# Weight loads in pieces of four row blocks, and the gate projection evacuated bank by bank, in an eight-core attention and expert-mixture layer

## What is computed

```
q, k, v, s, g = x @ Wq, x @ Wk, x @ Wv, clip(x @ Ws), x @ Wg
o = scan over tokens of (q, k, v, s)          # per head
o = o * rsqrt(mean(o*o) + eps) * g_norm_weight
o = o * (g * sigmoid(g))                       # the gate
x = layernorm(x + o @ Wo)
h = relu(x @ W1 + b1); alpha = softmax(h @ W2 + b2)
x = layernorm(x + sum_k alpha_k * U_k (V_k x))
```

## Time and profile before

| | |
|---|---|
| median of 2 runs | 1934.78 us (1932.53 to 1937.03) |
| profiled execution, its own time | 1948.56 us |
| its span, first to last instruction, core 7 | 1947.0 us |
| spans of the eight cores | 1908.6 to 1947.0 us |
| TensorE busy | 1357.1 us, 70% of the span |
| VectorE, ScalarE, GpSimd busy | 532.6, 409.1, 292.5 us |
| bytes read from HBM | 237.45 MB |

### The profile page before, as it was taken

How to read it: one execution, slowest core, us unless ns; L and a number is a source line. 1 busy time by engine, 2 the same in 40 slices (tenths; PEclk the granted TensorE clock), 3 DMA queues, 4 the chain that set the end, 5 groups by cost and what they waited for, 6 DMA issues and landing times.

```text
span 1947.0 us, 18988 instructions; the slowest of 8 cores (1908.6 to 1947.0 us)
## 1 busy us (share of the span) xinstructions
PE 1357.1 (70%) x6800; PEld 653.6 (34%) x6800; DVE 532.6 (27%) x886; ACT 409.1 (21%) x552; POOL 292.5 (15%) x310
## 2 busy tenths in 40 slices
PE   3358989969985554778685658967555477868562
PEld 1124444434433333333232323423333333324231
DVE  2013232341002222343421372000222234342135
ACT  0000000001124444320200131102444432020013
POOL 2100000001011111442111102201111144211100
PEclk9669999989985555887676868978555587768686
DMA  9940100015114000559935249961300055984502
GB/s 182 179 76 22 44 22 22 22 44 108 23 24 64 0 1 1 87 87 182 201 72 86 34 88 228 160 96 27 61 1 1 1 87 87 181 156 76 87 1 87
DMA packets 62956, 146.27 MB, mean 75 GB/s; under 512 B 8976, under 2 KB 13456, under 8 KB 57488
## 3 DMA queue, kind: packets, MB, share of 16 engines
q0 software_dynamic: 56240, 102.91, 34.7%
q1 hardware_dynamic: 5472, 33.76, 5.1%
q10 hardware_dynamic: 1152, 8.39, 1.1%
HBM read 237.45 MB, written 8.39 MB: 126 GB/s over the span
## 4 chain that ended last, share of the span: by engine, by line
PE 46%; DMA 19%; DVE 14%; ACT 8%; issue 6%; POOL 4%; DVEq 1%; ACTq 0%; another core or an unknown queue 0%; POOLq 0%
PE fb L245 44%; DMA wvb<-wv 5%; DMA wob<-wo 4%; DMA wkb<-wk 3%; DMA w1b<-w 3%; PE tb L245 2%; POOL wbf L265 2%; DMA wsb<-ws 2%; ACT rbuf L265 1%; DVE x1bufs L265 1%; DMA wqb<-wq 1%; DVE msq L265 1%; DVE st L265 1%; DVE sm L265 1%; ACT wrw L265 1%
## 5 line engine op out<-in xcount | busy, mean ns | idle before, releaser
L245 PE MATMUL fb<-w1b,x2fm 128*128 128x512 bf16 x512 | 140.6, 437 | 33.5 <-DMA w1b<-w 33.5
L245 PE MATMUL fb<-wob,ofm 128*128 128x512 bf16 x512 | 141.4, 450 | 14.1 <-DMA wob<-wo 14.1
L245 PE MATMUL fb<-wvb,xpf 128*128 128x512 bf16 x512 | 119.9, 395 | 32.7 <-DMA wvb<-wv 32.7
L245 PE MATMUL fb<-wgb,xmf 128*128 128x512 bf16 x512 | 132.7, 426 | 2.9 <-DVE psf L265 2.9
L245 PE MATMUL fb<-wvb,xmf 128*128 128x512 bf16 x512 | 118.5, 393 | 16.5 <-DMA wvb<-wv 16.5
L265 DVE TENSOR_TENSOR okb<-fb,rbuf 128x256 f32<-128x256 f32 x32 | 13.6, 424 | 316.3 <-ACT rbuf L265 171.4
L245 PE MATMUL fb<-wsb,xpf 128*128 128x512 bf16 x256 | 72.9, 449 | 31.4 <-DMA wsb<-ws 18.2
L245 PEld LDWEIGHTS fb<-w1b,x2fm 128*128 128x128 bf16 x512 | 53.0, 107 | 113.4 <-issue 82.8
L245 PEld LDWEIGHTS fb<-wob,ofm 128*128 128x128 bf16 x512 | 56.7, 112 | 97.9 <-issue 95.3
L245 PEld LDWEIGHTS fb<-wvb,xpf 128*128 128x128 bf16 x512 | 50.6, 100 | 99.3 <-issue 45.0
L265 DVE TENSOR_TENSOR s1f<-s1f,fb 64x256 f32<-64x256 f32 (+1 forms) x48 | 24.1, 502 | 208.6 <-PE fb L245 206.9
(11 more groups left out here) (149 smaller groups left out, 1957.7 us busy)
## 6 DMA issues: line engine op xcount, KB each, us to landing
strip<-x_main SPq DMA_DIRECT2D x24, 1024.0 KB, 10.1
wgb<-wg POOLq DMA_DIRECT2D x32, 512.0 KB, 19.5
wob<-wo POOLq DMA_DIRECT2D x32, 512.0 KB, 21.8
w1b<-w POOLq DMA_DIRECT2D x32, 512.0 KB, 21.9
wsb<-ws POOLq DMA_DIRECT2D x16, 512.0 KB, 21.6
strip<-x_pre SPq DMA_DIRECT2D x8, 1024.0 KB, 7.2
wkb<-wk POOLq DMA_DIRECT2D x16, 512.0 KB, 24.4
wvb<-wv POOLq DMA_DIRECT2D x8, 1024.0 KB, 42.0
```

Of the source, the lines that this page charges most:

```text
L245: t.matmul(o, l, r, start=a, stop=b, is_transpose=(True if tpp else None)))
```

## The change

**Pieces.** The default of `per_dma` goes from 2 to 4 in both loaders, and a load takes `min(npc, 4)` semaphores instead of up to 8. Each load after the first three is now 4 DMAs of twice the size (`utb` one instead of two). The first three keep pieces of two blocks, but use four semaphores each, so that their fifth piece waits for their first.

**Gate stage.** `g_proj` calls `gemm` once per bank, so that all 16 blocks go into the first bank before the second is begun, and keeps a token per bank; `g_evac` copies each bank on its own token; `g_gate` applies SiLU in two instructions of 512 columns, each waiting for its own copy.

```
-        def load_w(name, dram, rows, cols, col0=0, ncols=None, per_dma=2,
+        def load_w(name, dram, rows, cols, col0=0, ncols=None, per_dma=4,
...
-            sems = [next_wsem() for _ in range(min(npc, 8))]
+            sems = [next_wsem() for _ in range(min(npc, 4))]
...
         def load_w_into(buf, dram, rows, cols, col0=0, ncols=None,
-                        per_dma=2, waits=()):
+                        per_dma=4, waits=()):
...
-            sems = [next_wsem() for _ in range(min(npc, 8))]
+            sems = [next_wsem() for _ in range(min(npc, 4))]
...
                 def g_proj(c):
                     bk = [FB[0], FB[1]] if c % 2 == 0 else [FB[2], FB[3]]
-                    mG_of[c] = gemm(xslc(c),
-                                    lambda k, g: wgb2.ap(0, 128, k * GV + g * 512,
-                                                         min(512, GV - g * 512)),
-                                    KC, bk, GV, waits=[xe_tok[c]], ktok=twg2)
+                    toks = []
+                    for b in range((GV + 511) // 512):
+                        cn = min(512, GV - b * 512)
+                        toks.append(gemm(
+                            xslc(c),
+                            lambda k, g, b=b, cn=cn: wgb2.ap(
+                                0, 128, k * GV + b * 512, cn),
+                            KC, [bk[b]], cn,
+                            waits=[xe_tok[c]] if b == 0 else (), ktok=twg2))
+                    mG_of[c] = toks
...
                 def g_evac(c):
                     bk = [FB[0], FB[1]] if c % 2 == 0 else [FB[2], FB[3]]
-                    gv = None
+                    gvs = []
                     for g in range((GV + 511) // 512):
                         cn = min(512, GV - g * 512)
-                        gv = vop(lambda v, g=g, cn=cn, bk=bk, c=c: v.tensor_copy(
-                            gsc2[c % 2].ap(0, 128, g * 512, cn),
-                            bk[g][0:128, 0:cn]),
-                            waits=[mG_of[c], gsc2_free[c % 2]]
-                            + gsc2[c % 2].birth)
+                        gvs.append(vop(
+                            lambda v, g=g, cn=cn, bk=bk, c=c: v.tensor_copy(
+                                gsc2[c % 2].ap(0, 128, g * 512, cn),
+                                bk[g][0:128, 0:cn]),
+                            waits=[mG_of[c][g], gsc2_free[c % 2]]
+                            + gsc2[c % 2].birth))
                     for g in range((GV + 511) // 512):
-                        bset(bk[g], gv)
-                    gv_tok[c] = gv
+                        bset(bk[g], gvs[-1])
+                    gv_tok[c] = gvs
...
-                    sg = sop(lambda s: s.activation(sgs.ap(0, 128, 0, GV),
-                                                    gsc.ap(0, 128, 0, GV),
-                                                    AF.Silu, bias=0.0,
-                                                    scale=1.0),
-                             waits=[gv_tok[c], sgs_free[0]] + sgs.birth)
+                    sg = None
+                    for g in range((GV + 511) // 512):
+                        cn = min(512, GV - g * 512)
+                        sg = sop(lambda s, g=g, cn=cn: s.activation(
+                            sgs.ap(0, 128, g * 512, cn),
+                            gsc.ap(0, 128, g * 512, cn),
+                            AF.Silu, bias=0.0, scale=1.0),
+                            waits=[gv_tok[c][g], sgs_free[0]] + sgs.birth)
```

## The result

| | before | after |
|---|---|---|
| median of all runs | 1942.08 us (1932.53 to 2012.22, 13 runs) | 1925.53 us (1913.04 to 2009.62, 15 runs) |
| ratio, 95% interval | | 0.9899 [0.9869, 0.993] |
| profiled execution, span | 1947.0 us (core 7) | 1919.7 us (core 2) |
| TensorE busy | 1357.1 us | 1333.9 us |
| GpSimd busy | 292.5 us | 230.3 us |

The change makes the kernel 1.0% faster, some 19.5 us of 1935. The forecast was +1.1 us. Ratios leave out executions in which one die ran at a lower clock; the profiled executions of the changed kernel (cores 0 to 3), of e8 (0 to 3) and of e13 (4 to 7) are of that kind, and on their other four cores the load times are within 2 us of those stated here for all eight.

What follows compares the result with a forecast made beforehand. The prediction took the stretches where TensorE waits for late weight loads as bound by bytes in flight. Terms of +6.6, -3.8 and -1.7 us summed to +1.1 on the median of 1934.78, so 1935.9 us, 8-in-10 range 1916 to 1954.

Steps and rivals of the forecast that it cites:

- A price per piece: Late loads: whether each DMA piece carries a cost of its own; taken as zero because the engines show no gap.
- term 1: Ends of late loads: last bytes land as before, but 4 more matmuls follow at five ends; +6.6 us, bounds 4.4 and 8.8.
- sign of being right: Late loads: the last pieces land within 2 us of their present distance from the first issue.
- sign for rival 1: The four loads in a row take less than 110 us instead of the present 117.
- Rival 1: Loads: a cost per piece that adds up, 19 us saved over 32 fewer pieces, giving 1916.9 us; chance 0.14.
- Rival 2: Eight exposed loads: large pieces move slower, 0.6 us per MB over 64 MB, 38 us, giving 1974 us; chance 0.08.
- Rival 3: Gate stage ends: the first bank's copy really goes out halfway, saving 8.9 us, giving 1928.7 us; chance 0.10.
- Term 2: POOL's wgb issues ahead of the scan: four replace eight at 0.93 us each; -3.8 us for two scans, bounds -5.6 and 0.
- Term 3: Gate stage ends: first SiLU of 512 columns runs beside the second copy, 0.43 us at each of four; -1.7 us.
- Cost nothing: The gate's bank-by-bank matmul order and the waits inside the first three loads were claimed to add no time.

Runs made afterwards that it cites:

- e8: The changed kernel with only the late loads in pieces of one block: 0.9956 of before, the four loads in a row at 117.2 us.
- e13: The changed kernel with the wo loads alone reading adjacent rows: 0.9952 of before, wob's second columns at 49.8 and 47.3 us.
- e3: The kernel before with sixteen load semaphores instead of eight, same pieces of two blocks: 1.0018 of before, the four loads in a row at 118.3 us.
- e1: The kernel before with the change of the loads alone (pieces of four blocks, four semaphores): 0.9896 of before, the four loads in a row at 111.4 us.
- e9: The kernel before with each piece of two blocks taking blocks eight apart: 1.0079 of before, the four loads in a row at 123.9 us.
- e10: The changed kernel with each piece of four blocks taking blocks four apart: 1.0424 of before, the four loads in a row at 144.0 us.
- e14: The kernel before, pieces of two blocks, each partition reading adjacent rows: 0.9947 of before, the four loads in a row at 112.7 us.
- e5: The changed kernel with pieces of eight blocks except in the first three loads: 0.9871 of before, the four loads in a row at 111.3 us.
- e16: The kernel before with 24 loads of w1's second columns put in front, in eight patterns: neighbouring blocks two 31.0, four 28.1, eight 27.4 us a load.
- e2: The kernel before with the gate stage's change alone: 0.9983 of before, the four loads in a row at 118.1 us.
- e11: The changed kernel with pieces of four blocks in the first three loads too: 0.9902 of before.
- e6: The changed kernel with the last piece of each load after the first three cut in two: 0.9879 of before.
- e4: The kernel before with pieces of one block except in the first three loads: 1.0143 of before, the four loads in a row at 113.8 us.
- e15: The changed kernel with e7's order on VectorE and adjacent rows in the loads of e14, four blocks a piece: 0.9904 of before.
- e7: The changed kernel with VectorE's gsc copies of the next chunk ahead of the ofm copies: 0.975 of before.

## Why the prediction was wrong

**"A price per piece … I take zero": this step failed.** Not because a piece has a price. It failed one step earlier, at "the last bytes land at the same time in both kernels" in term 1 and "the change moves the same bytes", which set the gain of the transfers to zero. The bytes are the same and the rate is not: the late loads came 18 us earlier in all. The argument for zero was the full DMA share. But the share says nothing of the rate: in e3's window it is 9 tenths at 68 GB/s as at 213. The number in the same row, 161 GB/s, and the 2.49 us between two landings, which for 512 KB is 211 GB/s, the rate of a core alone in e1 and e3, were the sign that a quarter of the rate was lost to something. The prediction saw the gap and asked only whether it was a cost per piece. Its own sign of being right, last pieces within 2 us of their old distance, failed (117.3 to 111.9 us on the slowest cores), while its sign for rival 1, less than 110 us, was not met either. Why the memory serves one grouping of rows faster than another stays open.

**Rival 1** gave 1916.9 us, near the result of 1915.3, by luck, for a reason that the runs refute: its price per piece would have made e8 slower than it was, and left e9, e10 and e14 where they had been. **Rival 2** (longer lists are slower) is refuted by e5 and e16. **Rival 3** did not happen: the gsc copies stand behind the ofm copies as before.

**Term 1, the last piece.** The bursts are there: 8 matmuls in 3.57 us where 4 took 1.86, +1.7 us at an end at the slow rate; where the clock is at its upper level 8 take 1.89. That lies inside the bounds of 0.88 to 1.76. It was forecast at +6.6 us and is hidden in a larger gain. One end can be seen: from the first wkb issue to the gate's load the stretch fell from 170.7 to 165.8 us (medians; e1 166.0), 4.9 where the last landing came 6.9 earlier, so 2 us were given back.

**Term 2, issues ahead of the scan.** Right in its mechanism, a little small. Timeline of core 7, which answers to the earlier trace rows:

```profile
570.32 2.97 POOL L233 DMA_DIRECT2D wgb<-wg  x4 [105.83 <-ACT qtm L265]
...
571.57 0.59 ACT L265 CAST arw<-fb 128x512 bf16<-128x512 f32 x1
573.27 1.20 POOL L265 TENSOR_TENSOR abf<-arw,lmb 128x512 bf16<-128x512 bf16 x1
574.62 0.37 PE L245 MATMUL fb<-s1b,kqfm 64*128 64x64 bf16 x4 [3.28 <-POOL abf L265]
```

An issue of four blocks costs 0.74 us, not the 0.93 taken from b1sb: 5.64 - 2.97 is 2.67, and the scans are 2.6 and 2.2 us shorter, together 4.8 against 3.8.

**Term 3, SiLU in two.** Right in mechanism and size. The end of the gate stage, core 7, answers to the earlier trace rows:

```profile
864.00 0.95 DVE L265 COPY ofm<-tb 128x512 bf16<-128x512 bf16 x2 [2.57 <-PE tb L245]
865.05 1.49 DVE L265 COPY gsc<-fb 128x512 f32<-128x512 f32 x2
865.89 0.63 ACT L265 ACTIVATE sgs<-gsc 128x512 f32<-128x512 f32 x1 [5.93 <-DVE gsc L265]
866.68 0.63 ACT L265 ACTIVATE sgs<-gsc 128x512 f32<-128x512 f32 x1 [0.17 <-DVE gsc L265]
867.55 1.23 DVE L265 TENSOR_TENSOR otb<-obs,sgs 128x1024 bf16<-128x1024 f32 x1 [1.02 <-ACT sgs L265]
```

From gsc to otb are 2.50 us, before 2.93: the 0.43 of the forecast, and 0.63 us for 512 columns as the straight line gave. The four gate stages of a core add up to 173.6 to 175.3 us (medians) in before, e1, e3, e9 and e14, which have the old gate, and to 172.1 to 173.1 in the changed kernel, e2, e5, e8, e10, e11 and e13 (169.3 in e6). e2's 0.9983 has 1.7 us (0.9991) in its interval.

**Cost nothing.** At the start nothing new shows: from the first weight load's issue to the first wqb issue were 459.4 us and are 458.3, and the last wvb piece landed at 120.3 to 122.0 us and lands at 119.8 to 122.3. The waits inside the first three loads are covered.

**The sum by what was measured.** Loads -18, bursts +6.6 (by the forecast), scans -4.8, SiLU -1.7: -18 us. The eighteen stages between POOL's issues give -16.9 in the two profiled executions, the ratio -19.5.

## What to carry to other kernels

A full DMA share did not say here that the engines moved what they can (161 GB/s in the earlier trace rows where 211 were seen undisturbed): put the GB/s of the stretch beside the GB/s of an undisturbed load, and when they differ, ask which memory is shared and with whom. When neighbouring cores load large weights nearly at once, try the grouping of rows in a piece as a knob of its own, measured on all cores and in the kernel, because its effect was neither monotone in the size nor the same for each weight. And an evacuation per bank helps only if the order on the evacuating engine lets it go early; look at what stands ahead of it there.

## What was not expected of the hardware

- Loads of the same count and size of pieces and the same row length took 28 to 35 us for 4 MB, by which rows one piece takes together: two blocks 28.1 (adjacent rows), 31.0 (neighbouring), 34.1 us (distant), four blocks 28.1, 28.1 and 34.9 (e16).
- In the kernel pieces of one and of two blocks pass alike, four and eight alike, with a step between (four loads in a row 117 to 119 against 111 to 112). By themselves one block takes 29.5 us and two take 31.0; with the neighbours 19 to 21 us apart the four loads in pieces of one took 113.8 (e4).
- A neighbour that starts at the same moment costs 6 to 8 us of a 4 MB load in pieces of two (33 against 25 to 27 us) and 3 to 5 in pieces of four (29 to 30 against 25 to 26). The offset of neighbours was seen in the runs and not set on purpose; the loads by themselves show the effect of the rows, not that of the offset.
- Adjacent rows helped w1, wk, wv and wq in pieces of two, made wo of the first half slower by 3 us in pieces of two and by 8 in pieces of four, and in pieces of four made the four loads in a row slower too (114.1 in e15, 111.3 in e7). Why is open.
